# Half the convolution and the B, C, z projections behind the gating on TensorE; delta projection and softplus behind the gelu run; expert mix one unit later

## The reference

```
h = layernorm(x) * (1 + ca) + sa
xc, z = split(h @ in_proj.T)                       # 256 channels each
u = silu(causal_conv4(xc) + conv_b)
dt, Bm, Cm = split(u @ x_proj.T, [8, 24])
delta = softplus(dt @ dt_w.T + dt_b)
for t: state = state * exp(delta_t * A) + delta_t * u_t * B_t;  y_t = sum(state * C_t)   # 16 states
x = x + ga * (((y + u * D) * silu(z)) @ out_proj.T)
h = layernorm(x) * (1 + cb) + sb
w = top-2 of softmax(h @ router_w + router_b), 8 experts
x = x + gb * (gelu(h @ sw1 + sb1) @ sw2 + sb2 + sum_e w_e * (gelu(h @ rw1_e + rb1_e) @ rw2_e + rb2_e))
```

## Time and profile before

| | |
|---|---|
| three timed runs | 771.5, 773.55, 773.56 us; median 773.55 us |
| the profiled execution | 772.12 us, of which its span is 770.3 us |
| VectorE busy | 601.4 us (78%) |
| TensorE busy | 616.5 us (80%, ends of matmuls modelled) |
| ScalarE busy | 464.2 us (60%) |
| GpSimd busy | 322.5 us (42%) |
| DMA engines | mean 101 GB/s |

### The profile page before, as it was taken

One profiled execution on the slowest core, in us unless ns is written; L12 is line 12 of the kernel. 1 busy time (PEld: TensorE's weight loads), 2 busy tenths in 40 slices (PEclk: granted clock), 3 DMA queues, 4 the chain that ended last, 5 costly groups with the idle time before them and its releaser, 6 DMA issues.

```text
span 770.3 us, 9958 instructions
## 1 busy us (share of the span) xinstructions
PE 616.5 (80%) x3454; PEld 473.8 (62%) x3454; DVE 601.4 (78%) x701; ACT 464.2 (60%) x765; POOL 322.5 (42%) x172
## 2 busy tenths in 40 slices
PE   6565477799969996998969996999789856995697
PEld 4224344678456964777557954787467835794476
DVE  4298997979887997979797988889896998595301
ACT  2579534796368744996378745876479605831352
POOL 1025454435553554535443564436542554344000
PEclk9878569799969998799979997899979957997599
DMA  6403343123421233122431252313412332300000
GB/s 196 183 39 129 112 172 117 65 101 119 154 109 56 110 137 126 68 97 112 154 109 55 110 188 75 110 55 127 178 55 110 110 137 109 123 1 15 0 1 14
DMA packets 26367, 77.79 MB, mean 101 GB/s; under 512 B 2817, under 2 KB 17234, under 8 KB 18130
## 3 DMA queue, kind: packets, MB, share of 16 engines
q1 hardware_dynamic: 25842, 76.75, 27.2%
q10 hardware_dynamic: 480, 0.43, 0.2%
HBM read 74.55 MB, written 2.62 MB: 100 GB/s over the span
## 4 chain that ended last, share of the span: by engine, by line
PE 46%; DVE 25%; issue 11%; ACT 11%; POOL 4%; DMA 1%; ACTq 0%; DVEq 0%; POOLq 0%
DVE state L1079 13%; PE psum L513 8%; PE psum L486 7%; POOL state L412 4%; DVE psum L1070 4%; PE psum L603 4%; PE psum L604 3%; PE psum L605 3%; PE psum L560 3%; PE psum L635 3%; ACT h L902 2%; ACT decay L772 2%; PE psum L539 2%; PE psum L531 2%; PE psum L582 2%
## 5 line engine op out<-in xcount | busy, mean ns | idle before, releaser
L412 POOL TENSOR_TENSOR state<-state,bc 128x1024 f32<-128x1024 f32 x128 | 302.3, 2361 | 361.7 <-DVE psum L1070 361.2
L1079 DVE TENSOR_TENSOR_SCAN state<-decay,psum 128x1024 f32<-128x1024 f32 x128 | 291.9, 2280 | 11.0 <-PE psum L486 1.9
L486 PE MATMUL psum<-ident,state 128*128 128x128 f32 x1024 | 150.3, 296 | 42.5 <-POOL state L412 42.5
L772 ACT ACTIVATE decay<-delta,a_neg 128x511 f32<-128x511 f32 x256 | 163.0, 710 | 16.7 <-DVE state L1079 16.5
L486 PEld LDWEIGHTS psum<-ident,state 128*128 128x128 f32 x1024 | 130.4, 155 | 57.8 <-POOL state L412 49.0
L1070 DVE TENSOR_TENSOR psum<-bc,du 128x1024 f32<-128x1024 f32 x128 | 157.6, 1231 | 4.0
L635 PE MATMUL psum<-down_w,h 128*128 128x128 f32 x1024 | 127.2, 278 | 6.3 <-DVE gT_mix L1178 6.3
L635 PEld LDWEIGHTS psum<-down_w,h 128*128 128x128 f32 x1024 | 119.1, 192 | 15.9 <-DVE gT_mix L1178 9.4
L902 ACT ACTIVATE h<-psum,vec 128x512 f32<-128x512 f32 x144 | 96.7, 687 | 15.2 <-PE psum L605 13.9
L513 PE MATMUL psum<-h_sb,conv_in_wT 128*128 128x512 f32 x128 | 63.0, 641 | 17.7 <-ACT h_sb L782 15.4
L603 PE MATMUL psum<-h_hi,up_hi 128*128 128x512 f32 x144 | 65.5, 455 | 2.5 <-ACT h L902 2.5
(11 more groups left out here) (135 smaller groups left out, 617.1 us busy)
## 6 DMA issues: line engine op xcount, KB each, us to landing
bc<-bc_rows SPq DMA_DIRECT2D x64, 1024.0 KB, 4.7
x_sb<-_attn_hidden_states_dram SPq DMA_DIRECT2D x9, 256.0 KB, 2.9
out_dram<-out_sb SPq DMA_DIRECT2D x8, 256.0 KB, 2.4
x<-_attn_hidden_states_dram SPq DMA_DIRECT2D x7, 256.0 KB, 3.1
h<-in_L_ffn_rw_dram SPq DMA_DIRECT2D x1, 1024.0 KB
bc_rows<-rows SPq DMA_DIRECT2D x8, 64.0 KB, 2.1
h<-in_L_wmod_dram ACTq DMA_DIRECT2D x1, 384.0 KB
h<-in_L_attn_in_proj_w_dram SPq DMA_DIRECT2D x1, 256.0 KB, 4.6
```

Source lines behind the costliest of these rows:

```text
L412: pool.tensor_tensor(state[:, u % STATE_RING, :, :], state[:, u % STATE_RING, :, :], bc[:, pair % BC_RING, 1, first:first + NU, :], ALU.mu ...
L486: last = nc.tensor.matmul(Y[q][:, t * P:(t + 1) * P], state[:, u % STATE_RING, s, t * P:(t + 1) * P], ident[:, :], start=False, stop=(u in ...
L772: last = nc.scalar.activation(decay[:, r, s, 1:L], delta[:, b.p, q, 1:L], ACT.Exp, scale=a_neg[:, q, k:k + 1])
L1079: nc.vector.tensor_tensor_scan(state[:, u % STATE_RING, :, :].rearrange("p n t -> p (n t)"), decay[:, u % DECAY_RING, :, :].rearrange("p n ...
```

## The change

On TensorE, `conv_in` for q = 1 is cut into two halves of two taps. The first stands behind `g_transpose`, in front of `out_proj`, and the second behind `out_proj`; `x_proj` and the second `z_proj` follow behind `y_add(b, 0)`. `dt_proj` stands behind the 18 `up`. Three `y_add` stand among the `up` in place of two. The waits follow the PSUM banks: `up` now waits for the z gating, `dt_proj` for the last gelus of A[0] and A[1], and the first two `down` for `softplus_abs`. On ScalarE, `g_rows` and `att_rows` come in front of `x_silu(n, 1)`, one pair of decays comes in front of `h2_rows`, and `softplus_relu` and `softplus_abs` stand between the last gelu and `weights_out`, with `softplus_exp` behind it; `h_rows(m)`, `mix_scaled`, `skip_term` and the decays of n change places. On VectorE `make_delta` moves from behind unit 7 to behind the scan of unit 9, and the mix blocks move by one unit.

```
-MIX_AT = {8: (0,), 9: (1,), 10: (2,), 11: (3, 4), 12: (5,), 13: (6, 7)}
+MIX_AT = {9: (0,), 10: (1,), 11: (2, 3), 12: (4, 5), 13: (6, 7)}
...
             def dt_proj(n, a):
                 pe.wait_ge(bcdt_done, n.i + 1)
                 for q in range(Q):
-                    pe.wait_ge(zs_done, 2 * n.i + q + 1)
+                    if a:
+                        pe.wait_ge(gelu_done, M_UP * a.i + M_UP - 2 + q)
+                    else:
+                        pe.wait_ge(zs_done, 2 * n.i + q + 1)
...
-                if j < 2:
+                if j < 2 and n:
+                    pe.wait_ge(sp_abs, Q * n.i + j + 1)
+                elif j < 2:
                     pe.wait_ge(gelu_done, M_UP * a.i + M_UP - 2 + j)
...
                     for k in range(M_UP):
                         gelu(a, k)
+                if n:
+                    softplus_relu(n)
+                    softplus_abs(n, a)
+                if a:
                     weights_out(a)
                 if n:
+                    softplus_exp(n)
                     softplus_log(n)
...
+                if m:
+                    h_rows(m)
+                if a:
+                    mix_scaled(a, 4)
+                    mix_scaled(a, 5)
                 if n:
                     skip_term(n)
                     decays(n, 0)
                     decays(n, 1)
-                if m:
-                    h_rows(m)
-                if n:
-                    decays(n, 2)
-                if a:
-                    mix_scaled(a, 4)
-                    mix_scaled(a, 5)
-                if n:
-                    decays(n, 3)
                 if a:
                     mix_scaled(a, 6)
                     mix_scaled(a, 7)
+                if n:
+                    decays(n, 2)
+                    decays(n, 3)
+                if a:
                     acc_rows(a)
```

More of the change, by code:

```diff
@@ L501, in x_transpose, with conv_in @@
                 last.then_inc(xT_done, 1)
-            def conv_in(n, q):
+            def conv_in(n, q, taps=range(KC)):
                 if q == 0:
@@ L511, in conv_in @@
                         pe.wait_ge(sp_abs, Q * n.i)
-                for k in range(KC):
+                for k in taps:
                     last = nc.tensor.matmul(A[q], conv_in_wT[:, q, k, :], h_sb[:, k:k + L],
                                             start=(k == 0), stop=(k == KC - 1))
-                last.then_inc(conv_done, 1)
+                if k == KC - 1:
+                    last.then_inc(conv_done, 1)
             def z_proj(n, half):
@@ L547, in g_transpose @@
                 if n:
[L548 removed]
+                    pe.wait_ge(h_done, n.i + 1)
                 else:
@@ L668, in slots @@
                     z_proj(n, 0)
-                    x_proj(n)
-                    z_proj(n, 1)
                 if a:
@@ L674, in slots @@
                 if n:
-                    dt_proj(n)
+                    conv_in(n, 1, range(2))
                 if a:
                     out_proj(a)
+                if n:
+                    conv_in(n, 1, range(2, KC))
+                if a:
+                    att_transpose(a)
                 if b:
@@ L680, in slots @@
                     y_add(b, 0)
-                if a:
-                    att_transpose(a)
+                if n:
+                    x_proj(n, a)
+                    z_proj(n, 1)
                 if b:
@@ L685, in slots @@
                 if a:
-                    x1_transpose(a)
-                    router(a)
+                    x1_transpose(a, n)
                 if b:
                     y_add(b, 2)
+                if a:
+                    router(a)
                 for k in range(M_UP):
@@ L692, in slots @@
                         up(a, n, k)
-                    if b and k in (6, 14):
-                        y_add(b, 3 + k // 14)
+                    if b and k in (4, 11, 16):
+                        y_add(b, 3 + (4, 11, 16).index(k))
+                if n:
+                    dt_proj(n, a)
                 if a:
@@ L697, in slots @@
                     shared_down(a)
-                    down(a, 0)
-                if b:
-                    y_add(b, 5)
-                if a:
-                    down(a, 1)
+                    down(a, n, 0)
                 if b:
                     y_add(b, 6)
-                for u in range(8, UN - 2):
+                if a:
+                    down(a, n, 1)
+                if b:
+                    y_add(b, 7)
+                for u in range(9, UN - 2):
                     for j in MIX_AT[u]:
                         if a and j + 2 < DOWNS:
-                            down(a, j + 2)
+                            down(a, n, j + 2)
                         if a:
                             mix_add(a, j)
-                    if m and u == 10:
+                    if m and u == 11:
                         x_transpose(m, n, a)
@@ L801, in skip_term, with z_gate @@
                                          scale=vec[:, ROW_D + q:ROW_D + q + 1]).then_inc(skip_done, 1)
[L803 to L804 removed]
+            def z_gate(n, j):
+                if j == 0 and not (isinstance(n.i, int) and n.i < 2):
                     act.wait_ge(gT_done, n.i - 1)
+                act.wait_ge(z_done, 2 * n.i + j + 1)
                 zs = z_silu[:, n.p, :, :].rearrange("p t c -> p (t c)")
[L807 to L810 removed]
+                nc.scalar.activation(zs[:, j * 512:(j + 1) * 512], A[j],
+                                     ACT.Silu).then_inc(zs_done, 1)
             def bcdt_rows(n):
@@ L908, in slots @@
                     x_silu(n, 0)
+                    z_gate(n, 0)
+                if a:
+                    g_rows(a, n)
+                    att_rows(a)
+                if n:
                     x_silu(n, 1)
                     bcdt_rows(n)
-                    z_gate(n)
-                if a:
-                    g_rows(a, n)
-                if n:
-                    softplus_relu(n)
-                if a:
-                    att_rows(a)
-                if n:
-                    softplus_abs(n, a)
-                    softplus_exp(n)
+                    z_gate(n, 1)
                 if a:
                     load_exp_table(a)
+                if b:
+                    decays(b, AHEAD)
+                if a:
                     h2_rows(a)
                 if b:
-                    decays(b, AHEAD)
                     decays(b, AHEAD + 1)
@@ L1243, in slots @@
                     scan(b, 7)
-                if n:
+                if n and not b:
                     make_delta(n)
-                    if isinstance(n.i, int) and n.i == 0:
-                        split_up_weights()
+                if n and isinstance(n.i, int) and n.i == 0:
+                    split_up_weights()
                 for u in range(8, UN):
@@ L1258, in slots @@
                         scan(b, u)
+                    if n and b and u == 9:
+                        make_delta(n)
                     if n and u == 12:
```

28 lines of the change are left out of this document (12 added, 16 removed).

## The result

The changed kernel takes 838.78 us (median of four runs, 833.3 to 842.19) beside 773.41 us for the kernel before in the same job: a ratio of 1.0845, 95% interval 1.0776 to 1.0914. It is slower, as forecast, but by 65 us where 12 were forecast, and far outside the range of 775 to 797. The profiled execution took 841.29 us.

What follows compares the result with a forecast made beforehand. VectorE was taken to set the time, so only its waits could change. Five stages +6.6, late start +1.7, slow out-projections +4.2, fill +1, stage without m +1.9, without n -2.9: 772.1 + 12.5 = 784.6, stated as 785 us; range 775 to 797.

Steps and rivals of the forecast that it cites:

- Gate: VectorE's gate_y starts 7.3 us after the scan of unit 15 ("+7.3") instead of 9.6, a gain of 2.3.
- Residual: Out-projection: VectorE ready at +15.65, TensorE at +15.4, so no wait at the high clock; +17.1 at the low one.
- three slow `out_proj`: Out-projections on TensorE at the low clock: three at 1.4 us each, +4.2 us in the sum.
- Gelu run: First gelu at +31.4; 14.0 us to weights_out plus 0.85 for a third y_add; last gelu done at +46.2.
- Rival (2): TensorE's low clock spreads: all six out-projections slow (+4.2 more), 1.5 us in six gelu runs (+9): 798 us; chance 0.18.
- The step that failed: From weights_out at +49.2, 3.66 us to the first down and 2.0 to its end; VectorE waits 6.8 us.
- End of the stage: Units behind the first mix block: 29.8 us, plus a wait of 1.8 for the late finish; stage 86.5 us.
- M: Start of the first mix block on VectorE, forecast at +54.9; "M+x" is x us after it.
- late start: A term of +1.7 us in the sum for the whole execution.
- (4): Rival: short wait at the first mix block, M at +51.5, each stage gains 2 us net: 762 us; chance 0.07.
- (5): Rival: the change moves waits only, gating gain equals mix loss: 773 us; chance 0.07.
- (3): Rival: finish not late because the mix block chain closes faster; five stages lose 1.8 us each: 776 us; chance 0.12.

Runs made afterwards that it cites:

- e5: Changed kernel, order untouched, plus ten overwritten matmuls on TensorE between the last gelu and shared_down: 810.63 us, ratio 1.0487.
- e4: Changed kernel with skip_term put in front of h_rows of batch m: 815.1 us, ratio 1.0562.
- e11: e9 with one y_add among the up moved behind the first down, plus the six overwritten matmuls of e12: 758.79 us, ratio 0.9817.
- e6: Changed kernel with the edits of e3 and e4 together: 781.27 us, ratio 1.0098.
- e1: Changed kernel's new gating order alone; softplus, dt_proj, make_delta and mix blocks as in the kernel before: 787.1 us, ratio 1.0198.
- e12: Changed kernel, order untouched, plus six overwritten matmuls ahead of the router and between the third and fourth up: 828.3 us, ratio 1.0713.
- e9: e6 plus weights_transpose and weights_out in mid gelu run, acc_rows ahead of two decays: median 774.1 us, ten runs in two groups (774 to 775, 762 to 769).
- e3: Changed kernel with weights_out directly behind the last gelu, ahead of relu and abs: 796.96 us, ratio 1.0346.
- e13: Changed kernel, order untouched, with the overwritten matmuls of both e5 and e12, sixteen in all: 809.73 us, ratio 1.0469.

## Why the prediction was right and wrong

The direction, the early gate, the wait at the mix block and the end of the wait for the Ln were right. The size was wrong, and one wait was missed. Step by step, in the stage from 499.74 us, which was to last 86.5 and lasted 95.8:

- **Gate**: +7.3 forecast, +7.5 measured (507.22), wait 0.28. Right in five of six stages. In the stage from 400.62, which opens the second pass of the loop, the gate came at +11.5 where 9.0 were forecast: TensorE idled 3.37 us there, and the convolution behind the idle took 6.54 us, where in the kernel before it idled 2.34 and took 3.70. `make_delta`'s wait for the Ln: none, right. `weights_out` 3.0 us behind the last gelu: 3.1, right.
- **Residual**: "two taps 1.75", so +15.65 "if the clock is high". It came at +17.9: `g_transpose` (1.97 us, forecast 0.9) and the two taps (3.44) ran at the low level and then `out_proj` at the high one (1.88). 2.1 us. The low clock was expected at `out_proj` itself; it sat in front of it. The three slow `out_proj` of the sum did not come in these stages.
- **Gelu run**: "from first gelu to `weights_out` is 14.0 us" plus 0.85. The start was right (2.5 us late, with the residual and the gate), the run took 16.2 us to the last gelu's end in place of 14.8, with the first five `up` at the low level, 15 matmuls of 0.63 us or more where the kernel before has seven. 1.4 us. Rival (2) had this term, at 1.5 us, but with a chance of 0.18.
- **The step that failed: "from `weights_out` to the first `down` it is 3.66 us, and 2.0 more to its end."** Both are prices at the high level, taken over from a place where TensorE had idled 1.04 us. The change puts four evacuations in front of `weights_out`, TensorE idles 2.10, and from the start of `weights_out` to the mix block it is 9.6 us in place of 5.7, since `shared_down` and the first `down` run at the low level. 3.9 us in this stage, 3.4 to 4.6 in the six stages, 25 in all. e5 shows it by itself.
- **End of the stage**: forecast 29.8 and a late `finish` of 1.8, measured 33.0. `acc_rows` came where it was put (M+29.4, forecast 29.7), but `finish` does not wait in the loop, because VectorE is later still. `skip_term` does that harm: I counted it only among what delays `acc_rows` (at M+18.6 and later), and did not ask who reads it. It ends at 585.2, M+22.6; `delta_x` behind the scan of unit 12 wants it about 3 us earlier. The mechanism was missed; its price is 1.4 net of the forecast. Removing the wait, net of what `finish` then waits, is worth 14 us (e4).

These terms give 0.2 + 2.1 + 0.2 + 1.4 + 0.1 + 3.9 + 1.4 = 9.3 us, which is the difference of 95.8 and 86.5. But this stage is the shortest of the five, which last 95.8 to 99.1 us, and the stage without m, forecast at 84.7, took 96.3. The same terms over all six, each against its forecast: `weights_out` to mix block 25 us, gelu run to `weights_out` 15, gate to first gelu 9, gate 5, end of stage 11. That is 65 us. The forecast had put 5.9 of it into the late start and the three slow `out_proj`, and the first stages, forecast at +1, took 1.5 less than before. So 57 us remain, the difference of the forecast 784.6 and the profiled 841.3; the last two stages each came out within about 0.3 us of the forecast.

Two readings in the prediction are off, neither with weight. The end of a stage adds up to 29.6 and not 29.8 (28.94 - 3.7 + 4.4). And the three waits named at its start are 33.7 of the 45.7 us in which VectorE did not work in those four stages, three quarters and not nearly all.

The rivals: (2) was nearest, the low clock spreads, but it put the cost in `out_proj` and in the gelu run and none in `shared_down` and `down`, where the largest part was. (4) and (5) are out; the wait at M is long. (3) is right that VectorE does not wait for `finish`, but for another reason than it gives: the chain of mix blocks did not close faster. Of the prediction's signs of being wrong one came true: the clock differs between stages. In the five stages of one order the mix block comes 54.0 to 57.3 us behind the gate. The Trainium skill, "TensorE: Matmul & The Clock Gate", section "What's actually happening", says that the throttled state is the default and activity releases it. The prediction used this for `out_proj` alone. The trace agrees with it at `shared_down` and `down`, and e5 and e11 agree too: more matmuls, less time. How long an idle brings the low level back is not shown here: 0.77 us in e6 were followed by it, 2.40 in e11 were not. The other rule weighed, the drain of 1380 ns at a table switch that the prediction cites, does not show: in e1 `h2_rows` ends at 485.86, the exp load of 1.28 us starts at 485.88 and its exp at 487.17.

What stays open: what, beside the idle just before, decides whether a stretch is low, and so why e5 and e12 don't add and why e4 and e6 changed the level at places that their edits left alone; and the true time of e9.

## What to carry to other kernels

Where VectorE waits for a matmul that a change puts behind an idle of TensorE, price it twice, at the level that its row shows and at the other one; here that was 3.9 us of 9.3 in the stage shown. For each instruction that is moved ask not only whom it delays but who reads its result: `skip_term` was free as a delay and dear as a result. And a version that loses may hold a gain: with five further edits it is 1.8% faster than the kernel it lost to.

## What was unexpected in the hardware

Matmuls whose results nobody reads paid for themselves: ten of them brought 838.8 to 810.6 us (six more gave nothing on top), and six brought 765.4 to 758.8. Yet the same six made the kernel before 6 us slower. And the same idle does not always have the same effect: in e3 an idle of 0.77 us ahead of `shared_down` was followed by matmuls at the high level, in e6 by the low one; in e11 an idle of 2.40 ahead of the fourth `up` left the following matmuls at 0.39 us, and in e13 one of 2.39 at the same place was followed by matmuls of 0.63 from the third on.
